# The last stage's table lookup, taken out of its own block and spread over a feed forward and three attentions

## The reference

```python
def _ghost_linear(x, idx, lut):
    w = lut[idx]
    return jnp.einsum('bsh,oh->bso', x, w)
gate = _ghost_linear(x, gate_idx, lut)
up = _ghost_linear(x, up_idx, lut)
h = jax.nn.silu(gate) * up
return _ghost_linear(h, down_idx, lut)
```

## Time and profile before

| | |
|---|---|
| median of 3 runs | 4135.32 us (4134.88 to 4137.27) |
| the profiled execution's own time | 4134.45 us |
| its span, from first to last instruction | 4132.6 us |
| TensorE matmul busy | 3217.2 us (78%) |
| VectorE busy | 1970.5 us (48%) |
| ScalarE busy | 1126.1 us (27%) |
| GpSimd busy | 563.8 us (14%) |
| mean granted TensorE clock | 0.874 |

### The profile page before, as it was taken

The page is one execution under the profiler, slowest core; times in us unless marked ns, Lnnn a source line. Parts: engine busy times, 40 slices in busy tenths (PEclk is TensorE's granted clock), DMA queues, the critical chain, the costliest instruction groups (busy, mean ns, idle before and its releaser), DMA issues. The chain is left out here.

```text
span 4132.6 us, 52343 instructions
## 1 busy us (share of the span) xinstructions
PE 3217.2 (78%) x19426; PEld 2419.0 (59%) x19426; DVE 1970.5 (48%) x4588; ACT 1126.1 (27%) x2319; POOL 563.8 (14%) x713
## 2 busy tenths in 40 slices
PE   6999899989999558888781888768787876006999
PEld 5777688867666334556661666356565654005887
DVE  4444432134443453135756666355556564994111
ACT  2223311113322102112220222133333344772000
POOL 0010132211100000001310000021212121001222
PEclk8999899988999768899995999889898988557999
DMA  2000200010000302120001000300000002000000
GB/s 75 2 2 2 88 1 0 1 49 2 2 1 1 105 1 82 41 87 1 0 3 79 0 0 0 102 1 2 1 2 1 2 1 85 0 0 0 11 11 21
DMA packets 45111, 88.97 MB, mean 22 GB/s; under 512 B 6723, under 2 KB 10307, under 8 KB 44229
## 3 DMA queue, kind: packets, MB, share of 16 engines
q1 hardware_dynamic: 44454, 85.60, 5.9%
q0 software_dynamic: 416, 0.10, 0.0%
HBM read 81.60 MB, written 4.19 MB: 21 GB/s over the span
## 5 line engine op out<-in xcount | busy, mean ns | idle before, releaser
L602 DVE CUSTOM_DVE_ANT_0 bank<-bank,a_causal 128x384 f32<-128x384 f32 (+3 forms) x512 | 235.9, 524 | 156.1 <-PE bank L711 156.1
L95 PE MATMUL bank<-f_xT_hi,f_w_hi 128*128 128x512 f32 (+1 forms) x704 | 276.2, 392 | 5.7 <-DVE f_w_lo L1081 4.1
L96 PE MATMUL bank<-f_xT_hi,f_w_lo 128*128 128x512 f32 (+1 forms) x704 | 275.7, 392 | 0.0
L97 PE MATMUL bank<-f_xT_lo,f_w_hi 128*128 128x512 f32 (+1 forms) x704 | 275.5, 391 | 0.0
L527 ACT ACTIVATE a_PT<-bank 128x512 f32<-128x512 f32 (+1 forms) x384 | 174.4, 526 | 238.1 <-PE bank L724 237.9
L1130 PE MATMUL bank<-ident,f_xn 128*128 128x128 f32 x128 | 18.4, 306 | 282.6 <-DVE f_xn L1069 282.6
L897 ACT ACTIVATE bank<-f_bit,f_lut,f_step 128x512 f32<-128x512 int32 x264 | 190.7, 767 | 85.7 <-DVE bank L934 47.6
L1130 PEld LDWEIGHTS bank<-ident,f_xn 128*128 128x128 f32 x128 | 17.2, 160 | 284.3 <-DVE f_xn L1069 283.5
L1101 DVE TENSOR_TENSOR f_sg<-bank,f_sg 128x512 f32<-128x512 f32 (+1 forms) x44 | 30.4, 691 | 286.9 <-PE bank L97 286.9
L2175 PE MATMUL bank<-a_KT,a_QT 128*128 128x256 f32 (+1 forms) x512 | 144.0, 390 | 20.2 <-ACT a_QT L1972 20.2
L1099 DVE SCALAR_TENSOR_TENSOR f_sg<-bank,f_us,f_sg 128x512 f32<-128x512 f32 x44 | 33.0, 751 | 264.2 <-PE bank L97 264.2
(11 more groups left out here) (441 smaller groups left out, 8394.0 us busy)
## 6 DMA issues: line engine op xcount, KB each, us to landing
f_w_raw<-in_f_w SPq DMA_DIRECT2D x11, 768.0 KB, 13.1
f_idx<-in_f_idx SPq DMA_DIRECT2D x11, 768.0 KB, 12.4
x_res<-in_x SPq DMA_DIRECT2D x4, 1024.0 KB, 9.5
m_piece<-in_m_wq SPq DMA_DIRECT2D x2, 2048.0 KB, 11.5
m_piece<-in_m_wo SPq DMA_DIRECT2D x2, 2048.0 KB, 9.4
m_piece<-in_m_w_gate SPq DMA_DIRECT2D x2, 2048.0 KB, 10.9
m_piece<-in_m_w_up SPq DMA_DIRECT2D x2, 2048.0 KB, 7.8
m_piece<-in_m_w_down SPq DMA_DIRECT2D x2, 2048.0 KB, 11.1
```

Of the source, the lines that this page charges most:

```text
L95: pe.matmul(out, w[0], x[0], start=first, stop=False, skip_group_check=True)
L96: pe.matmul(out, w[1], x[0], start=False, stop=False, skip_group_check=True)
L97: return pe.matmul(out, w[0], x[1], start=False, stop=last, skip_group_check=True)
L602: last = dve.tensor_tensor_reduce(out=ps[J.bank(key)][:, col:col + n], in0=ps[J.bank(key)][:, col:col + n], in1=causal[:, T - n:T], scale= ...
```

## The change

The lookup's block is gone. Its 33 pieces are cut into 66 parts of 128 x 256, each is looked up earlier, stored to a tensor in device memory (`table_w`), and f3 loads its weights from there as f0 loads its own, with the split into high part and remainder in its first batch.

Parts 0 to 43 are done in f0, one for each of its 4 x 11 chunks, with the same tree of leaves and picks, now in SBUF and with masks of one byte, taken from the lowest byte of each index. Parts 44 to 65 are done by GpSimd in a0 (9), a1 (9) and a2 (4), as a sum over the 16 table values of (index == k) * value, in 31 steps for a part. In a0 and a1 some 4.4 steps stand at each `exp` entry of the order, in a2 some 2.6 at each of its 48 `S`, `PT` and `PV` entries.

`attention32` keeps one V instead of two, and f0 keeps two buffers of normalised tiles (`NX`) instead of four; f3 keeps four.

```diff
+def table_steps(prog, pool, start, end):
+    for n in range(start, end):
+        i, s = n // TABLE_STEPS, n % TABLE_STEPS
+        idx, total = prog.table_idx[i % 2], prog.table_sum[i % 2]
+        if s == 0:
+            pool.wait_ge(*prog.table_in[i % 2](0, 16 * (i // 2 + 1)))
+            if i >= 2:
+                pool.wait_ge(*prog.table_out[i % 2](0, 16 * (i // 2)))
+            pool.tensor_scalar(total[:, :], idx[:, :], 0.0, prog.table_lut[:, 0:1], ALU.is_equal, ALU.mult).then_inc(prog.table_step.sem, 1)
+        elif s == 1 or s % 2 == 0 and s < TABLE_STEPS - 1:
+            k = 1 if s == 1 else s // 2 + 1
+            if n >= 3:
+                pool.wait_ge(*prog.table_step(0, n - 2))
+            pool.tensor_scalar(prog.table_term[k % 3][:, :], idx[:, :], float(k), prog.table_lut[:, k:k + 1], ALU.is_equal,
+                               ALU.mult).then_inc(prog.table_step.sem, 1)
+        else:
+            k = 15 if s == TABLE_STEPS - 1 else (s - 1) // 2
+            pool.wait_ge(*prog.table_step(0, n if k == 15 else n - 1))
+            pool.tensor_tensor(total[:, :], total[:, :], prog.table_term[k % 3][:, :], ALU.add).then_inc(prog.table_step.sem, 1)
+
+def tree_moves(prog, sp):
+    first, last = TABLE_TREE
+    sp.dma_start(prog.table_lut[:, :], prog.ins["f3_lut"].partition_broadcast(P)).then_inc(prog.table_lut_in.sem, 16)
+    for h in range(last + 1):
+        if h < last:
+            sp.wait_ge(*prog.tree_mask(0, 4 * h)) if h else None
+            sp.dma_start(prog.tree_idx[:, :], table_part(prog.ins["f3_idx"], h)).then_inc(prog.tree_in.sem, 16)
+        if h:
+            sp.wait_ge(*prog.tree_pick(0, 7 * h))
+            sp.dma_start(table_part(prog.table_w, h - 1), prog.tree_value[(h - 1) % 4][:, :]).then_inc(prog.tree_out.sem, 16)
+    sp.wait_ge(*prog.tree_out(0, 16 * last))
+
+def tree_masks(prog, dve, h):
+    if h >= TABLE_TREE[1]:
+        return
+    dve.wait_ge(*prog.tree_in(0, 16 * (h + 1)))
+    if h >= 2:
+        dve.wait_ge(*prog.tree_pick(0, 7 * (h - 1)))
+        dve.wait_ge(*prog.tree_leaf(0, 8 * (h - 1)))
+    low = prog.tree_idx[:, :].bitcast(U8).rearrange("p (n four) -> p n four", four=4)
+    for k in range(4):
+        dve.tensor_scalar(prog.tree_bit[h % 2][k][:, :], low[:, :, 0], 1 << k, None, ALU.bitwise_and).then_inc(prog.tree_mask.sem, 1)
+
+def tree_leaves(prog, act, h):
+    act.wait_ge(*prog.tree_mask(0, 4 * h + 1))
+    for k, (to, picked) in enumerate(((0, 0), (1, 0), (2, 0), (3, 0), (1, 1), (3, 2), (2, 3), (3, 4))):
+        if 7 * h + picked:
+            act.wait_ge(*prog.tree_pick(0, 7 * h + picked))
+        if k == 3 and h:
+            act.wait_ge(*prog.tree_out(0, 16 * h))
+        act.activation(prog.tree_value[(h + to) % 4][:, :], prog.tree_bit[h % 2][0][:, :], ACT.Identity, bias=prog.table_lut[:, 2 * k:2 * k + 1],
+                       scale=prog.tree_step[:, k:k + 1]).then_inc(prog.tree_leaf.sem, 1)
+
+def tree_picks(prog, dve, h):
+    dve.wait_ge(*prog.tree_mask(0, 4 * h + 4))
+    for n, (keep, other, bit, leaves, picked) in enumerate(((0, 1, 1, 2, 0), (2, 3, 1, 4, 0), (0, 2, 2, 0, 2), (1, 3, 1, 6, 0), (2, 3, 1, 8, 0),
+                                                            (1, 2, 2, 0, 5), (0, 1, 3, 0, 6))):
+        ...
+        dve.copy_predicated(prog.tree_value[(h + keep) % 4][:, :], prog.tree_bit[h % 2][bit][:, :],
+                            prog.tree_value[(h + other) % 4][:, :]).then_inc(prog.tree_pick.sem, 1)
...
 attention32, SP, behind the stage's loads:
+            table_moves(prog, sp, *share)
 attention32, GpSimd, behind roots(0):
+            table.begin(pool, 1 if split_y else 3)
             for kind, at, k in ORDER:
+                if kind == "exp":
+                    table.run(pool)
...
 feed_forward, SP:
+            if not share:
+                sp.wait_ge(*prog.tree_out(0, 16 * TABLE_TREE[1]))
+                for i in range(2):
+                    sp.wait_ge(*prog.table_out[i](0, 16 * (TABLE_PARTS - TABLE_TREE[1]) // 2))
+            for j in range(NJ):
+                sp.dma_start(W_raw[:, j * 3 * D:(j + 1) * 3 * D].rearrange("p (m d) -> p m d", m=3),
+                             weights[j].rearrange("m p d -> p m d")).then_inc(w_in[j].sem, 16)
+            if share:
+                tree_moves(prog, sp)
 feed_forward, ScalarE, ahead of the loop over batches:
+            if share:
+                act.wait_ge(*prog.table_lut_in(0, 32))
+                act.wait_ge(*prog.tree_ready(0, 1))
 in the loop, behind silu and weight(j + AHEAD):
+                    if share:
+                        tree_leaves(prog, act, i)
 feed_forward, VectorE, ahead of the loop over batches:
+            if share:
+                dve.wait_ge(*prog.table_lut_in(0, 32))
+                two = prog.table_lut[:, :].rearrange("p (k two) -> p k two", two=2)
+                dve.tensor_tensor(prog.tree_step[:, :], two[:, :, 1], two[:, :, 0], ALU.subtract).then_inc(prog.tree_ready.sem, 1)
+                tree_masks(prog, dve, 0)
 in the loop, behind the multiply and weight(j + AHEAD):
+                    if share:
+                        tree_picks(prog, dve, b * NJ + j)
+                        tree_masks(prog, dve, b * NJ + j + 1)
                     if j == 2 and b + 1 < NB:
                         statistics(b + 1)
                     if j == 6 and b + 1 < NB:
-                        normalise(b + 1)
+                        normalise(b + 1, range(NX))
                 if b + 1 < NB:
+                    if NX < TT:
+                        normalise(b + 1, range(NX, TT))
                     rest(b + 1)
```

More of the change, by code:

```diff
@@ L33 @@
 SLOTS = 64
+SBUF_END = 229368
+U8 = mybir.dt.uint8
+TABLE_COLS = 256
+TABLE_STEPS = 31
+TABLE_PARTS = 66
+TABLE_TREE = (0, 44)
 class Count:
@@ new lines, with __init__, begin, run @@
+class TableShare:
+    def __init__(self, prog, parts, calls):
+        self.prog, self.first, self.last, self.calls, self.n = prog, parts[0], parts[1], calls, 0
+    def begin(self, pool, stage):
+        pool.wait_ge(*self.prog.table_lut_in(0, 16 * stage))
+    def run(self, pool):
+        a, total = self.first * TABLE_STEPS, (self.last - self.first) * TABLE_STEPS
+        table_steps(self.prog, pool, a + self.n * total // self.calls, a + (self.n + 1) * total // self.calls)
+        self.n += 1
@@ L317, in attention32 @@
     K, _ = prog.pair(name + "_K", [P, KC, T])
-    V = [prog.sb(f"{name}_V{i}", [P, TT, KC * P], F32) for i in range(2)]
+    V = prog.sb(name + "_V", [P, TT, KC * P], F32)
     WIDTH = (512, 512, 256)
@@ L456, in _ @@
             roots(0)
+            table = TableShare(prog, share, len([1 for e in ORDER if e[0] == "exp"]))
+            table.begin(pool, 1 if split_y else 3)
             for kind, at, k in ORDER:
-                if kind == "T":
+                if kind == "exp":
+                    table.run(pool)
+                elif kind == "T":
                     pool.wait_ge(*read((kind, at, k)))
@@ L847, in feed_forward @@
     xT, _ = prog.pair(name + "_xT", [P, DC, T])
-    xn = [prog.sb(f"{name}_xn{i}", [P, D], F32) for i in range(TT)]
+    NX = 2 if share else TT
+    xn = [prog.sb(f"{name}_xn{i}", [P, D], F32) for i in range(NX)]
     h = [prog.pair(f"{name}_h{i}", [P, T])[0] for i in range(2)]
@@ L854, in feed_forward @@
         down_s = prog.sb(name + "_ds", [P, D], F32)
-    if table:
-        W_idx = prog.sb(name + "_idx", [P, NJ * 3 * D], I32, offset=at + NJ * 3 * D * 4)
-        prog.at = early
-        lut = prog.sb(name + "_lut", [P, 16], F32)
-        step = prog.sb(name + "_step", [P, 8], F32)
-        bit = [[prog.sb(f"{name}_bit{i}_{k}", [P, D], I32) for k in range(4)] for i in range(2)]
     def piece(j, m, i):
@@ L959, in feed_forward @@
+    weights = ins[f"{name}_w"] if share else prog.table_w
+    n_const = 3 if scaled else 0
+    out_done = prog.count("out_done")
     order_T = (1, 3, 0, 2)
@@ L1023, in weight @@
             def weight(j):
-                if not table and j < NJ:
+                if j < NJ:
                     act.wait_ge(*w_in[j](0, 16))
@@ L1137, in gate_up @@
                         pe.wait_ge(*read("T", b, tt))
-                if b == 0 and not table:
+                if b == 0:
                     pe.wait_ge(*c_wlo(0, j + 1))
@@ L1172, in feed_forward @@
         c.advance(n)
-    if not table:
-        for j in range(NJ):
-            w_in[j].advance(16)
-        c_whi.advance(NJ)
-        c_wlo.advance(NJ)
+    for j in range(NJ):
+        w_in[j].advance(16)
+    c_whi.advance(NJ)
+    c_wlo.advance(NJ)
     if scaled:
@@ L1299, in _ @@
             pool.wait_ge(*c_const(0, 32))
+            table = TableShare(prog, share, 3 * NT)
+            table.begin(pool, 4)
             for kind, b, k in ORDER:
-                if kind == "qk":
+                if kind in ("S", "PT", "PV"):
+                    table.run(pool)
+                elif kind == "qk":
                     n = b * NQK + k
```

162 lines of the change are left out of this document (63 added, 99 removed).

## The result

The changed kernel takes 4014.7 us (median of 4 runs, 4010.9 to 4020.6) against 4135.5 before: a ratio of 0.971 [0.969, 0.973], 121 us less. The prediction was 3927, with a range to 3980: the sign was right, and 88 us of the forecast gain did not come. The profiled execution took 4010.89 us with a span of 4009.1.

The account below looks back on a forecast made before the run. TensorE was taken to be busy almost throughout, except 271 us at the lookup ahead of the last stage. Terms: -268.6 + 11.2 + 9.6 + 20.7 + 2.3 + 9 + 7.5 = -208.3, giving 3927 us, own range 3912 to 3945, wider 3890 to 3980.

Parts of the forecast that it names:

- the price of GpSimd's step: In the attentions: a compare-multiply takes 0.50 us and an add 0.78, a mean step of 0.64.
- the prediction's own formula: First attention: a unit takes 4 x 4.36 steps at their price plus 1.98 us, against 14.9; the excess counts 16 times.
- GpSimd binds the first attention: Rival, chance 0.10: at 0.9 us a step a unit takes 17.7 against 14.9, costing 45 us, total 3968.
- The bound of fit: First attention: GpSimd's runs fit its 12.92 us idle between output splits while a step stays under 0.74 us.
- The second attention: Its first cast waits for the table at the stage start, costing 7.5 us; its other waits are long, costing 0.
- The block's gain: Ahead of the last stage: without the lookup the first product comes at 3491.6 instead of 3760.13, gaining 268.6 us.
- The feed forward: First feed forward: start 11.2, first pass 9.6, batch ends 20.7 and stage end 2.3 us lost; predicted +43.8.
- the start's wait: First feed forward: the first hidden chunk is ready at 517.4 where TensorE wanted it at 508.64, 8.8 us.
- the end: End of the first feed forward: the residual adds wait for the last selects, 2.3 us.
- first pass: First feed forward: chunks that also carry a weight subtract exceed the loop's period on VectorE, costing 9.6 us (0 to 20).
- cheap cover: Rival, chance 0.15: selects do not share with GpSimd and the clock holds; costs 33 us, time 3900.
- slower than before: Rival, chance 0.02: GpSimd's steps in the attentions cost 208 us at 1.5 us a step; slower from there.

Follow-up runs that it names:

- the multiply alone: The changed kernel with each of GpSimd's compare-multiplies replaced by a multiply by a constant; 3974.5 us, ratio 0.961.
- the first two points of the table: The changed kernel with each compare-multiply made a copy (step 0.61, 3960.4 us) or a multiply by a constant (step 0.82, 3974.5 us).
- The placed kernel: The changed kernel with GpSimd's steps in the first and second attention moved away from the casts of the next batch's turned input; 3917.4 us, ratio 0.948.
- without the selects: The fastest attention order of GpSimd's steps (3917.4 us), without masks, leaves and selects in the first feed forward, transfers and two row buffers kept; 3880.4 us, ratio 0.938.
- the kernel with the batch-end edit: The 3917.4 us kernel with third and fourth normalised tiles made ahead of the last chunk's selects in the first feed forward; 3911.5 us, ratio 0.946.

## Why the prediction was wrong

**The term that failed** is the price of GpSimd's step: "I take 0.50 and 0.78 [...]: 0.64". It is 0.98 in the stage, all of the error in the compare-multiply (1.15 us at the least against 0.50). The value taken, 0.50, lay between half and whole of a cast of 512 columns. The width was not the mistake (the cast of 256 columns takes 0.40, less than the 0.50 taken), but the cast is no neighbour of a tensor_scalar. The prediction's upper bound for the mean step, 0.93, was too low as well. The dearer of its two rows, the two-operand instruction, would not have been enough either: at 0.78 for every step, which the prediction had for the add, the formula below gives 10 us.

**With the measured price the prediction's own formula comes near the result.** At 0.9 a step the rival "GpSimd binds the first attention" had 45 us. At 0.98 it gives 17.4 x 0.98 + 1.98 - 14.9 = 4.1 a unit, 66 in sixteen; measured beyond the start: 65.0. It had a chance of 0.10 and should have been the forecast. Its mechanism is a backlog: nobody waits for an output split inside a batch, so GpSimd may fall behind from unit to unit, and the debt is paid where the next batch's casts stand, and once more at the last split (13.4 us). That the total fits so well is luck: at 0.82 the formula gives 22 and 35.4 was measured. It also leaves out the short pauses between steps (125.14 to 126.36 and on to 127.18 in the timeline above: 1.22 and 0.82 from start to start for 1.14 and 0.73 busy). With a start-to-start time of 1.03 a step it gives 80 for the 65.0, and for the multiply alone (0.93 and 0.81, a mean of 0.87) it gives 36 for the 35.4, so neither reading fits both points. The bound of fit, read from an idle of 12.92 us, lies nearer 0.64 than 0.74. One reason, argued and not tested, is that in a batch's last unit four casts of 0.61 stand between the steps as well, which the 12.92 does not contain. At my own price of 0.64 the loss would have been about 10 beyond the start (an estimate between the first two points of the table) where I had 5. By that estimate some 55 of the 60 us missed here hang on the price and 5 on the bound.

**The second attention** was costed at its start alone, since "its other waits are long". The start is 8.3 (7.5 forecast). The rest, 18 us, is three batch ends. TensorE's wait for the remainder of the turned input over the stage, before the change and after:

```profile
PE bank L95 <- DVE a_xT_lo L564: 6.9, 3, 2.3
```

```profile
PE bank L101 <- DVE a_xT_lo L706: 22.0, 3, 8.0
```

These are 6.7, 7.3 and 8.0 us where each was 2.31 before, and the granted clock is 0.50 in the 2 us behind the first two of them (1129 to 1131, 1260 to 1262). GpSimd has no output splits there and idles long, yet four or five steps stand between one cast and the next; long idle time upstream does not help an instruction that is placed behind work in its own queue. The placed kernel takes that away. This step failed as a mechanism, not by size.

**What was right.** The block's gain, 268.2 for 268.6. The feed forward, 40.4 for 43.8, and its parts: the start's wait 9.3 for 8.8; the second and third batch 6.7 and 7.0 us longer for 6.9 each; the end 2.0 for 2.3; the first batch with start and first pass 24.8 for 27.7. Prices: a select at a median of 0.45 for 0.42, a leaf 0.60 for 0.55, a mask 0.285 for 0.36. No second function table is loaded. VectorE and GpSimd do take turns at a select; in the timeline of the changed kernel, at the first batch's last chunk,

```profile
671.46 1.26 POOL L1069 TENSOR_TENSOR f_h_lo<-f_sg,f_h_hi 128x512 fp32r<-128x512 f32 x1
...
671.60 2.02 DVE L395 COPY_PREDICATED tree_value<-tree_bit,tree_value 128x256 f32<-128x256 uint8 x2 [0.66 <-ACT tree_value L381]
```

two selects beside GpSimd's subtract take 2.02, where two alone take 0.90. The rule that the prediction named from the page "SBUF — State Buffer" of the Trainium skill holds for them too.

The first attention's start cost 4.3 for 4. The 512-wide attention took 1.0 for 0. (The rival "cheap cover" is added up wrongly in the prediction: 8.8 at the start, 9.9 at the batch ends, 2.3, 9 and 7.5 are 37.5 and not 33, which makes it 3904. Nothing else hangs on it.)

**The rival "slower than before"** needs 121 us more. At the top the first attention loses 193 us per us of step and the second 45 (6.9 us more from 0.82 to 0.98), so the break-even would lie at 0.98 + 121/238 = 1.5 us a step. It is an extrapolation of two points. That it agrees with the 1.5 given is partly chance, since the prediction counted from 0.74, in one attention, and against a larger gain.

## What to carry to other kernels

A price for an instruction that the trace does not hold must come from the same kind of instruction on the same engine; here twice the width took 1.5 to 1.75 times as long, while another kind at the same width took nearly three times. If only other kinds are there, the dearest of them is no upper bound, and a rival that hangs on the price deserves more than a chance of 0.10. When background work is dealt out over an engine's queue, sum the debt over the whole cycle, and look at what stands behind the dealt work at the point where somebody waits; the same 315 us of GpSimd's work cost 65 us beyond the start in one order and next to nothing in another. An idle engine is no proof of a free place: in the stage that picks rows GpSimd was idle, and the steps cost 21 us there, 7 of them in TensorE's waits for one kind of VectorE instruction that took longer beside GpSimd.

## What the runs showed that was not expected

GpSimd's tensor_scalar costs by the number of its operations and not by the type it reads: from 256 to 512 columns a copy grows by 0.21 us, one operation by 0.63, two by 0.85, a two-input add by 0.54. The Trainium skill's "GPSIMD Engine Reference" (Elementwise — side-by-side cycle accounting) has 1.03 cycles an element where the ports bind, about 1.8 for a tight loop as a best case, and 2.6 for a two-input tensor_tensor. An estimate with the 1.2 GHz of that section turns the differences here into 1.0 for the copy, 3.0 and 4.0 for one and two operations, and 2.5 for the add. The copy and the add agree with the page; the tensor_scalar takes 1.7 and 2.2 times the 1.8, and the measurement decides.

A stage that no edit touches moved by 7 to 14 us. The windowed attention takes 801.8 us before and 802.0 without the selects, but 809.1 after and 815.7 in the kernel with the batch-end edit. Two stretches of it, 100 us from its start, before and after:

```profile
2777.00:2877.00 100.00, 90.43 (x425) 63.53 (x424) 60.07 (x177) 44.88 (x129) 22.82 (x36) 1.00 0.01 1
```

```profile
2914.00:3014.00 100.00, 90.41 (x411) 62.55 (x410) 59.36 (x176) 43.81 (x128) 22.94 (x36) 0.97 0.00 1
```

At the same busy time TensorE gets through 411 instructions instead of 425; the granted clock is 0.97 instead of 1.00. Over the whole stage TensorE's same 2976 instructions are busy 634.9 us before, 640.2 after and 647.5 in the kernel with the batch-end edit, at mean granted clocks of 0.91, 0.90 and 0.89, while the busy times of the other engines agree within 0.6 us. So the difference is TensorE's clock. What decides it stays open; no run here was made for it. It sets how finely two single profiles can be compared in total, and it is why the differences above are read stage by stage.
